# The one-time setup's loads and order, and the first head's loads, stores and rotations in each attention stage

## What is computed

```
mod = silu(c) @ wmod                      # per layer: sa, ca, ga, sb, cb, gb
h = layernorm(x) * (1 + ca) + sa
# Hyena: up = h @ in_w; 3-tap conv; k = filter(z) * decay (3 sine layers);
#        y = irfft(rfft(v*x1) * rfft(k)) + v*x1*bias;  x += ga * ((y * x0) @ out_w)
# FFN:   weights alpha * sign(w), gelu;            x += gb * ffn(layernorm(x) ...)
# attention: q, k, v = h @ Wq, Wk, Wv; rope on q and k; causal softmax; x += ga * out @ Wo
# experts: top 2 by the first row's score;         x += gb * mean of two experts
```

## Time and profile before

| | us |
|---|---|
| median of 3 runs | 1931.47 |
| lowest and highest | 1931.16, 1936.39 |
| the profiled execution, whole | 1928.46 |
| its span in the profile | 1926.5 |
| busy in the span: PE, DVE, ACT, POOL | 1761.5, 1439.4, 999.4, 693.0 |
| first `in_w` product of batch 0, batch 1 | 109.44, 562.08 |

### The profile page before, as it was taken

One profiled execution on the slowest core, in us unless ns is written; L12 is line 12 of the kernel. 1 busy time (PEld: TensorE's weight loads), 2 busy tenths in 40 slices (PEclk: granted clock), 3 DMA queues, 4 the chain that ended last, 5 costly groups with the idle time before them and its releaser, 6 DMA issues.

```text
span 1926.5 us, 27319 instructions
## 1 busy us (share of the span) xinstructions
PE 1761.5 (91%) x9228; PEld 1426.0 (74%) x9228; DVE 1439.4 (75%) x2652; ACT 999.4 (52%) x2158; POOL 693.0 (36%) x717
## 2 busy tenths in 40 slices
PE   6678879999999969999999969999999996999998
PEld 3567767777877857777787767777787785777777
DVE  4468878887478777887568887888746888788754
ACT  1132456777441436767633426677734144777752
POOL 0023244544224144553324134444323314455422
PEclk9889989999999989999999988999999998999999
DMA  6320054343160053443161024435225005354311
GB/s 248 137 109 1 19 152 116 100 127 78 41 257 1 1 132 105 127 105 89 45 230 55 1 69 123 106 100 138 57 87 209 1 1 132 104 136 119 88 29 50
DMA packets 90127, 184.14 MB, mean 96 GB/s; under 512 B 28991, under 2 KB 43135, under 8 KB 86790
## 3 DMA queue, kind: packets, MB, share of 16 engines
q1 hardware_dynamic: 82694, 168.77, 29.9%
q10 hardware_dynamic: 7296, 13.63, 2.5%
HBM read 125.46 MB, written 46.94 MB: 89 GB/s over the span
## 4 chain that ended last, share of the span: by engine, by line
PE 70%; DVE 11%; ACT 5%; issue 4%; DMA 3%; POOL 2%; DVEq 2%; ACTq 1%; SPq 1%; POOLq 0%; another core or an unknown queue 0%
PE ps L436 10%; PE ps L559 8%; PE ps L579 7%; PE ps L581 6%; PE ps L602 6%; PE ps L600 6%; PE ps L599 6%; PE ps L442 5%; PE ps L772 4%; PE ps L693 3%; PE ps L648 3%; DVE oT L1199 2%; PE ps L585 2%; PE ps L514 1%; DMA mix<-inverse_scratch 1%
## 5 line engine op out<-in xcount | busy, mean ns | idle before, releaser
L1178 DVE CUSTOM_DVE_ANT_0 ps<-ps,mrow 128x128 f32<-128x128 f32 (+7 forms) x512 | 384.9, 765 | 115.2 <-PE ps L559 113.5
L1450 POOL TENSOR_TENSOR psplit<-pT,psplit 128x384 fp32r<-128x384 f32 (+3 forms) x320 | 301.9, 957 | 424.1 <-ACT psplit L893 419.0
L893 ACT ACTIVATE psplit<-ps 128x512 fp32r<-128x512 f32 (+3 forms) x768 | 373.1, 486 | 0.0
L892 ACT ACTIVATE pT<-ps 128x512 f32<-128x512 f32 (+3 forms) x512 | 256.3, 501 | 167.3 <-PE ps L585 88.0
L559 PE MATMUL ps<-khl,qhh 128*128 128x512 f32 (+3 forms) x768 | 252.3, 393 | 60.2 <-DMA qhh<-psplit 34.1
L579 PE MATMUL ps<-qhh,khl 128*128 128x512 f32 (+3 forms) x768 | 271.1, 353 | 7.8 <-ACT psplit L893 7.5
L581 PE MATMUL ps<-q,k 65*128 65x512 f32 (+3 forms) x768 | 267.9, 349 | 0.0
L599 PE MATMUL ps<-psplit,vhi 128*65 128x512 f32 (+3 forms) x768 | 264.0, 344 | 0.0
L602 PE MATMUL ps<-psplit,vhi 128*65 128x512 f32 (+3 forms) x768 | 259.5, 338 | 0.0
L600 PE MATMUL ps<-psplit,vlo 128*65 128x512 f32 (+3 forms) x768 | 259.0, 337 | 0.0
L559 PEld LDWEIGHTS ps<-khl,qhh 128*128 128x128 f32 x768 | 131.6, 201 | 79.3 <-issue 59.6
(11 more groups left out here) (200 smaller groups left out, 3305.1 us busy)
## 6 DMA issues: line engine op xcount, KB each, us to landing
qhh<-q_scratch SPq DMA_DIRECT2D x112, 256.0 KB, 4.9
q_scratch<-hrow SPq DMA_DIRECT2D x24, 1024.0 KB, 6.9
mix<-inverse_scratch SPq DMA_DIRECT2D x64, 256.0 KB, 3.5
q<-q_scratch SPq DMA_DIRECT2D x56, 256.0 KB, 4.3
Kf<-kf_scratch SPq DMA_DIRECT2D x3, 3072.0 KB, 17.3
khl<-k_scratch SPq DMA_DIRECT2D x24, 256.0 KB, 7.5
sgn<-sgn_scratch SPq DMA_DIRECT2D x6, 1024.0 KB, 10.0
x<-in_x SPq DMA_DIRECT2D x5, 1024.0 KB, 5.4
```

Source lines behind the costliest of these rows:

```text
L892: A(full(n)[:, 0:hi - lo], ps[:, b, 0:hi - lo], ACT.Exp, scale=SCALE)
L893: A(psplit[:, n % PRING, 0, 0:hi - lo], ps[:, b, 0:hi - lo], ACT.Exp, scale=SCALE)\
L1178: V.tensor_tensor_reduce(out=v, in0=v, in1=mrow[:, L - n:L], scale=1.0, scalar=-3e38, op0=ALU.add, op1=ALU.max, accum_out=mx[:, u % 2, i:i ...
L1450: G.tensor_tensor(psplit[:, n % PRING, 1, 0:m], full(n)[:, 0:m], psplit[:, n % PRING, 0, 0:m].bitcast(F32), ALU.subtract)\
```

## The change

Setup: ACT's queue takes a part of the loads; the two operands that filter layer 0 needs come first on either queue. The raw weights get four homes: `wmod0` stays in `spare`, `wmod1` goes to Kf's blocks 0 and 1, `in_w` to Kf's block 3, `wqkv` to `wo` and `rope` in two halves; `wo` and `rope` themselves are loaded once `wqkv` is split (`loaded_late`). The meeting and the clearing of semaphores are gone; setup and batches share one `Banks` object and counts with an offset (`MADE`). PE, DVE and ACT get another order, below. The x of batch 0 is loaded once. DVE gets a wait for `gate_stored` before its first spectrum product in each batch.

Attention: POOL adds for k = 0, 1, 2 (DVE for 3) once `hT` is complete; all rotations stand before all low parts; SP issues key and query loads of both halves first, then the other operands of head 0, then `load_next(0)`; `store_rest` and `load_next(1)` on ACT stand behind the arrival of the first rows, and two stores move to SP behind `load_maxima(0)`; `project_values(1)` stands before the row scores and `turn_maxima(0)` before `project(4)`; POOL's value lows wait for `rope_lo` 4; ACT asks for its exponential table ahead of the first exponential with an operation on one column.

PE, the setup from its first product to the first spectrum products: before, then now. `fw` are the filter's weights, `spare` (and now `Kf`) the raw modulation weights.

The diff, cut to its core:

```diff
@@ tensor
+            filtered(0)
+            modulation(0, (0, 1, 2))
+            filtered(1)
+            modulation(0, (3,))
+            gate(0)
+            filtered(2)
...
+            modulation(1, (0, 1, 2, 3))
...
+            gate(1)
+            pe.wait_ge(*at("loaded_windows", 16 * 3))
+            pe.wait_ge(*at("kern_done", NT // 2))
+            kernel_spectrum(0)
...
             for h in range(NHALF):
                 normed(0, h)
-            part_ends(pe, "tensor")
+            for m in range(1, NB):
+                kernel_spectrum(m)
...
+                project_values(1)
                 for i in range(NT):
                     score_rows(0, i)
+                turn_maxima(0)
                 project(4, QCOL + GQ * HD)
-                turn_maxima(0)
-                project_values(1)
@@ scalar
+            for dst, src in ((fw1[:, :], d["L0_attn_mlp_w1"]), (fb[:, 3:4], d["L0_attn_freq"])):
+                load(dst, src, allow_slow_non_contiguous=True).then_inc(s["loaded_first"], 16)
+            load(cT[:, :, :, :], d["cT"], allow_slow_non_contiguous=True).then_inc(s["loaded_c"], 16)
+            load(wmod[0], d["wmod0"]).then_inc(s["loaded_mod0"], 16)
+            load(w2T[:, :, :], d["w2T"]).then_inc(s["loaded_w2"], 16)
+            load(wmod[1], d["wmod1"]).then_inc(s["loaded_mod1"], 16)
+            load(in_raw, d["in_w"]).then_inc(s["loaded_in"], 16)
...
+                value_rows(0)
+                for k in range(4):
+                    high(k)
                 act.wait_ge(*at("rope_lo", 1))
                 value_rows(1)
+                act.wait_ge(*at("first_rows0", 16 * 4))
+                act.wait_ge(*at("first_rows1", 16 * 4))
+                store_rest(nc.scalar.dma_start, act, 0)
+                store_rest(nc.scalar.dma_start, act, 1)
+                load_next(nc.scalar.dma_start, 1)
+                turn_maxima(0)
+                A(rden[:, 0, 0:1], neghalf[:, 0:1], ACT.Exp)
@@ vector
+            copy_gate(1)
+            dve.wait_ge(*at("loaded_in", 16))
+            split([in_w[:, a, :, :] for a in range(2)], in_raw, s["raw_used"])
             for h in range(NHALF):
                 h_low(0, h)
-            part_ends(dve, "vector")
+            mix_spectrum(0)
+            for layer in range(2):
+                bound_gate(layer)
+            mix_spectrum(1)
+            dve.wait_ge(*at("loaded_qkv", 16 * 2))
+            for q in range(ND):
+                split([wqkv[:, a, q, :] for a in range(2)], qkv_raw[q], s["qkv_split"])
+            mix_spectrum(2)
...
+            mix_spectrum(3)
...
+                dve.wait_ge(*at("gate_stored", 16))
                 for i in range(NB):
                     multiply(0, i, Yf[i]).then_inc(s["y_dve"], 1)
@@ gpsimd
+                pool.wait_ge(*at("h_lo_done", (LN_ATT + 1) * NHALF * ND))
+                for k in range(3):
+                    rotate(k)
+                pool.wait_ge(*at("rope_lo", 4))
                 value_low(0)
-                rotate(2)
+                value_low(1)
                 rotate(4)
@@ sync
-            sp.wait_ge(bar, 4)
-            sp.sem_clear(range(nums[0], nums[-1] + 1))
+            sp.wait_ge(*at("qkv_split", 2))
+            for dst, src in ((wo[:, :, :], d["wo"]), (rope[:, :, :], d["rope"])):
+                dma(dst, src).then_inc(s["loaded_late"], 16)
```

More of the change, by code:

```diff
@@ L312, in adaln_hyena_binffn_gqa_moe @@
         freed = [sem(f"freed{i}") for i in range(8)]
-        cleared = list(s.values()) + ready + freed
-        nums = [q.num for q in cleared]
-        assert nums == list(range(nums[0], nums[0] + len(nums)))
-        now = {"batch": 0}
+        now = {"batch": SETUP}
         def at(name, n):
-            return s[name], n + now["batch"] * EACH.get(name, 0)
+            if now["batch"] == SETUP:
+                return s[name], n
+            return s[name], n + MADE.get(name, 0) + now["batch"] * EACH.get(name, 0)
         def m_loaded(u):
@@ L443, in sign_mm, with modulation @@
                 return i
-            def modulation(layer):
-                pe.wait_ge(*at("silu_done", 1))
-                pe.wait_ge(*at("loaded_raw", 16 * (layer + 1)))
-                b = bk.take(pe, ("modT", layer))
-                for n, kind in enumerate((0, 1, 3, 4)):
+            MOD_BANK, GATE_BANK = (2, 5), (3, 4)
+            KINDS = (0, 1, 3, 4)
+            def modulation(layer, some):
+                if some[0] == 0:
+                    pe.wait_ge(*at("silu_done", 1))
+                    pe.wait_ge(*at(f"loaded_mod{layer}", 16))
+                    bk.take(pe, ("modT", layer), at=MOD_BANK[layer])
+                b = bk.held(("modT", layer))
+                for n in some:
                     for dt in range(ND):
@@ L469, in _ @@
                 for h in range(NHALF):
-                    b = bk.take(pe, ("filter", layer, h))
+                    b = bk.take(pe, ("filter", layer, h), at=h)
                     w = fw1[:, :] if layer == 0 else fw23[:, layer - 1, :]
@@ L855, in _ @@
                 normed(0, h, modn)
-            part_ends(act, "scalar")
-            bk = banks["batch"]
+            for m in range(1, NB):
+                copy_spectrum(m)
             def high(k):
@@ L1325, in _ @@
                 turn_and_add(3)
-                low(2)
-                low(3)
+                for k in range(4):
+                    low(k)
                 for i in range(NT):
```

284 lines of the change are left out of this document (141 added, 143 removed).

## The result

The changed kernel takes **1882.5 us** (median of 4 runs, 1878.9 to 1884.4) where the kernel before, on the same chip, takes 1932.5 (4 runs, 1931.2 to 1936.4): ratio **0.9738**, 95% interval 0.972 to 0.9756. It is faster by 50.0 us.

A forecast was written before the change was run, and what follows sets the result against it. PE was taken as nearly always busy in the steady part, waiting on a chain in setup and on operands in attention's opening. 1926.5 - 35.3 (setup) - 19.2 (attention) = 1872.0, 1874.0 with 1.96 around the span; forecast 1875, range 1861 to 1893.

The follow-up runs named there:

- E3: The changed kernel with ACT issuing the three loads of the next head's rows ahead of its two stores: ratio 0.9776 to the kernel before.
- E5: The changed kernel with all four stores on SP's queue behind the load of head 0's maxima, ACT issuing only its three loads: ratio 0.9822 to the kernel before.
- E9: The changed kernel with the three loads of head 1's second half moved from ACT's queue to SP's, behind the maxima's load: 1879.4 us, ratio 0.9717.
- E12: E9 with E7's idle products, which nothing reads, ahead of head 0's first rows and the turn of its maxima: 1880.5 us, ratio 0.9731.
- E10: The changed kernel as it is, measured and profiled again beside E9 on the same chip: 1883.1 us, ratio 0.9739 to the kernel before.
- E1: The changed kernel's setup with the opening of attention of the kernel before: ratio 0.9773 to the kernel before.
- E2: The kernel before with only the new opening of attention, its setup kept old: ratio 0.9933 to the kernel before.
- E8: The changed kernel with the filter's first weight and freq issued behind cT and wmod0 on ACT's queue: ratio 0.9747 to the kernel before.
- E11: The changed kernel with all of the setup's loads issued by SP, in the order of need: ratio 0.9732 to the kernel before.
- E4: The changed kernel with the turn of head 0's maxima back behind project(4): ratio 0.9749 to the kernel before.
- E7: The changed kernel with idle products on PE, 24 ahead of head 0's first rows and 6 ahead of its maxima's turn: ratio 0.9752 to the kernel before.

## What to carry over

Where an operand of a few KB is on the path, count the bytes asked for before it on every queue, and not the time of the issuing engine: freeing that engine only exposed them (E3), and moving the stores behind it exposed the engine that waits to overwrite the stored tile (E5). Of a DMA that "may be late" list both who waits for its data and who wants to write over its source. When an order on one engine is changed, look at what slides forward on its neighbours, memsets too, and when a wait is taken away, price what it covered: here two waits and a low clock lay on top of each other. Taking the maxima's wait away gave 2.9 us in that stretch where 8 to 12 were expected (E9), and taking the low clock away as well gave 2.7 where 6 to 8 were (E12).

## What the runs showed of the chip

- **A DMA issue takes longer while much is in flight, on the other queue too.** A load of 128 KB took 0.6 us to issue in the rows' loads of every kernel with the new opening, 0.68 for the first two on ACT's queue with no store issued yet (E3), and 2.7 behind two stores of 768 and 512 KB (5.41 for two, after). SP's third load of the next head, on a queue without a store on it, took 2.88 in after, beside ACT's stores, and 1.45 in E5, without them.
- **The clock rises at different times in the same program.** Filter layer 2 took 2.19 us in after's first profile and 3.64 in its second (E10), 3.67 being the lower level; on the same products it took 1.90 in E3 and 3.64 in E1, whose setup is the same. `in_w` started at 70.7 to 73.9 in the ten profiles with that setup, and the two with 3.64 are the latest (72.8 and 73.9).
- **The opening of attention comes in two lengths.** From column scores to values every batch of E2, E8, E10 and E11 took 8.6 to 8.7 us; it was 9.2 to 12 where the products behind the scores ran at the low level (granted clock 0.55 from 221.5 to 224 in after), as in every batch of E3, E4 and E7, where the clock of this stretch was 0.57 to 0.83. E9 and E12 lie between, at a clock of 0.97 to 1.00: 8.8 to 9.8 us. In after's profile all but one batch were of the long kind, in its second profile (E10) none was. A difference of 4 us between two traces of one program is therefore ordinary here, and one trace of before and one of after set that stretch no better than that.
- **A DVE instruction beside a single-row memset on POOL took 1.98 us for 0.42**, with one tile and two columns of scalars as its inputs, 26 times out of the 26 that they started within 0.06 us of each other.
